# Flamingo-style gated cross-attention with a routed FFN on one core: root iterations on GpSimd, softmax quarters folded into ScalarE, a later fill of the sorted rows, other unit sizes and a new written-out order

## The reference, cut to what matters

```python
x = x + tanh(g_xattn[0]) * xattn(layernorm(x), ctx_768, ...)   # softmax(q k^T / sqrt(16)) v, then wo
x = x + tanh(g_ffn[0]) * ffn(layernorm(x), ...)
# layernorm: (x - mean) / sqrt(var + 1e-5)
# ffn: top1 = argmax of 2 gate scores per token
#   masked[e] = x for tokens of expert e, 0 for the others
#   sum over e of relu(masked[e] @ w1[e] + b1[e]) @ w2[e] + b2[e]     (256 -> 1024 -> 256)
#   + relu(x @ sw1 + sb1) @ sw2 + sb2                                 (shared layers)
```

## Time and profile before

| | us |
|---|---|
| runs before, median (lowest to highest) | 377.28 (376.28 to 381.96), 3 runs |
| the profiled execution: its own time | 374.43 |
| its span in the trace | 372.7 |
| PE busy | 337.0 (90% of the span) |
| DVE, ACT, POOL busy | 246.0, 213.1, 189.9 |

### The profile page before, as it was taken

How to read it: one execution, slowest core, us unless ns; L and a number is a source line. 1 busy time by engine, 2 the same in 40 slices (tenths; PEclk the granted TensorE clock), 3 DMA queues, 4 the chain that set the end, 5 groups by cost and what they waited for, 6 DMA issues and landing times.

```text
span 372.7 us, 7238 instructions
## 1 busy us (share of the span) xinstructions
PE 337.0 (90%) x2337; PEld 304.5 (82%) x2337; DVE 246.0 (66%) x560; ACT 213.1 (57%) x420; POOL 189.9 (51%) x207
## 2 busy tenths in 40 slices
PE   4997189899799999999999798999999999999990
PEld 4665168687698888898889687999999999999980
DVE  5569768888997997977596688632444544445440
ACT  1464488765676764737575375445466554765540
POOL 9194549873526637658252008624454534644342
PEclk9599569999999999999999999999999999999996
DMA  7999375617402242002224011021123112222120
GB/s 191 320 243 335 83 203 150 156 27 198 98 6 82 51 106 75 0 16 99 69 81 146 1 59 57 22 92 37 49 85 84 57 29 73 60 58 66 28 85 28
DMA packets 42935, 34.51 MB, mean 93 GB/s; under 512 B 19370, under 2 KB 40397, under 8 KB 42909
## 3 DMA queue, kind: packets, MB, share of 16 engines
q1 hardware_dynamic: 39210, 26.35, 26.5%
q0 software_dynamic: 2864, 7.17, 6.0%
q10 hardware_dynamic: 835, 0.67, 0.7%
HBM read 22.35 MB, written 12.35 MB: 93 GB/s over the span
## 4 chain that ended last, share of the span: by engine, by line
PE 54%; DVE 14%; SPq 7%; DMA 7%; issue 7%; ACT 4%; POOL 3%; POOLq 2%; DVEq 0%; ACTq 0%
PE y_ps L1360 21%; PE h_ps L1360 13%; PE s_ps L1360 9%; PE bank L1360 6%; DMA stage<-in_L_ffn_w 3%; SPq L522 3%; PE bank L1486 2%; DVE ew_lo L1259 2%; DMA stage<-in_L_ffn_sw 2%; DMA x_all<-in_x 2%; DVE rsum L1150 2%; SPq L447 2%; DVE other_sum L1118 1%; POOLq L659 1%; DVE smax L1132 1%
## 5 line engine op out<-in xcount | busy, mean ns | idle before, releaser
L1326 DVE TENSOR_TENSOR hT_lo<-h,hT_hi 128x256 fp32r<-128x256 f32 x72 | 33.4, 463 | 42.9 <-ACT h L999 42.7
L666 POOL TENSOR_TENSOR probs<-probs,rinv 128x616 f32<-128x616 f32 x32 | 39.2, 1229 | 36.6 <-DVE rinv L1154 35.7
L694 POOL TENSOR_TENSOR hT_lo<-h,hT_hi 128x512 fp32r<-128x512 f32 (+1 forms) x25 | 28.7, 1160 | 25.6 <-ACT h L916 25.5
L1360 PE MATMUL y_ps<-ew_hi,hT_hi 128*128 128x256 f32 x144 | 41.4, 288 | 0.0
L1360 PE MATMUL y_ps<-ew_hi,hT_lo 128*128 128x256 f32 x144 | 40.3, 280 | 0.0
L1360 PE MATMUL y_ps<-ew_lo,hT_hi 128*128 128x256 f32 x144 | 40.3, 280 | 0.0
L1360 PE MATMUL y_ps<-sw_hi,hT_hi 128*128 128x256 f32 x128 | 37.5, 293 | 1.8 <-POOL hT_lo L694 1.8
L996 ACT ACTIVATE hT_hi<-h_ps,vec_cols 128x256 fp32r<-128x256 f32 x36 | 17.1, 476 | 33.8 <-PE h_ps L1360 33.8
L1360 PE MATMUL bank<-pT,v_diag 128*128 128x256 f32 (+1 forms) x160 | 36.3, 381 | 0.0
L1360 PE MATMUL y_ps<-sw_hi,hT_lo 128*128 128x256 f32 x128 | 36.1, 282 | 0.0
L1360 PE MATMUL y_ps<-sw_lo,hT_hi 128*128 128x256 f32 x128 | 36.1, 282 | 0.0
(11 more groups left out here) (186 smaller groups left out, 1086.3 us busy)
## 6 DMA issues: line engine op xcount, KB each, us to landing
v_diag<-v_rows SPq DMA_DIRECT2D x8, 512.0 KB
stage<-in_L_ffn_w SPq DMA_DIRECT2D x4, 1024.0 KB, 6.1
sorted_dram<-empty_rows SPq DMA_DIRECT2D x10, 257.0 KB, 8.5
xs<-sorted_dram SPq DMA_DIRECT2D x10, 257.0 KB, 2.8
stage<-in_L_ffn_sw SPq DMA_DIRECT2D x2, 1024.0 KB, 6.1
x_all<-in_x SPq DMA_DIRECT2D x1, 1536.0 KB, 10.2
part_dram<-x_all SPq DMA_DIRECT2D x3, 512.0 KB, 2.9
k_dram<-probs SPq DMA_DIRECT2D x8, 154.0 KB, 5.5
```

The costliest lines, as they stand in the source:

```text
L666: nc.gpsimd.tensor_tensor(pq, pq, rinv[:, b % 2, k, :].unsqueeze(2).to_broadcast([P, HG, KEYS]), ALU.mult).then_inc(p_ready, 1)
L694: nc.gpsimd.tensor_tensor(hT[1][:, q % HB, 0:width], h32[:, q % 2, 0:width], hT[0][:, q % HB, 0:width], ALU.subtract).then_inc(h_lo_pool, 1)
L1326: nc.vector.tensor_tensor(hT[1][:, c % HB, 0:RTOK], h32[:, c % 2, 0:RTOK], hT[0][:, c % HB, 0:RTOK], ALU.subtract).then_inc(h_lo, 1)
L1360: return nc.tensor.matmul(out_, lhsT, rhs, start=start, stop=stop, **kw)
```

## The change

- The eight batches are grouped for the shared layers as 1, 1, 2, 2, 2 in place of 1, 2, 2, 2, 1.
- The Newton steps and the shift of the second layer norm (all five units) and of the third group of the first (twelve tiles) go from DVE to POOL. DVE keeps the statistics and the three instructions of the first guess. One root is 14 POOL instructions (12 for the steps, 2 for the shift), each waiting for the one before.
- For the 13 quarters in `FOLDED`, DVE does not subtract; it writes the negated maximum, and ACT takes the exponents straight from PSUM, one instruction of 77 columns for each of eight heads, with the maximum as bias. PE then waits for the exponents before it writes these banks again. The scale 1/4 moves into the queries.
- Of each unit's eight low parts two (chunks 1 and 7) are left on POOL in place of five.
- The fill of the sorted rows moves in SP's list from the front to behind `wd.2`; the zeros for the values are two steps with a semaphore each.
- All five lists are written anew; ten warm-up matmuls in place of eight. `wh.0` stands behind `ex.1.1` in ACT's list, where it stood behind `ex.0.1`. The context transposes `yt` stand ahead of the vectors' transpose `vt`.

In the diff, `PE_ORDER` and `ACT_ORDER` are cut to their first lines (and PE's last), and DVE's list is left out.

```diff
+POOL_ROOT = 4 * NEWTON + 2
...
-WARM = 8
-UNITS = [[0], [1, 2], [3, 4], [5, 6], [7]]
+WARM = 10
+UNITS = [[0], [1], [2, 3], [4, 5], [6, 7]]
...
-LO_ON_POOL = (2, 3, 4, 5, 7)
-SORTED_BANK = 1
+LO_ON_POOL = (1, 7)
+FOLDED = {0, 2, 11, 16, 20, 21, 22, 23, 26, 27, 28, 30, 31}
+SORTED_BANK = 0
 PE_ORDER = """
-    warm vt yt.0 yt.1 yt.2 yt.3 kp.0.0 kp.0.1 kp.1.0 in.0.0 kp.1.1 qy.0.1 vp.0 sc.0.0 sc.0.1 vp.1 in.1.0 vp.2
-    vp.3 sc.0.2 qy.1.1 sc.0.3 tn.0.0.0 tn.0.1.1 tn.0.2.0 tn.0.3.1 tn.0.4.0 in.2.1 sc.1.0 sc.1.1 qy.2.0 in.3.1
-    sc.1.2 sc.1.3 va.0.0 qy.3.1 sc.2.0 ou.0.0 in.4.1 sc.2.1 tn.1.0.0 tn.1.1.1 qy.4.0 tn.1.2.1 sc.2.2 tn.1.3.0
-    tn.1.4.1 in.5.0 sc.2.3 va.1.1 tn.2.0.0 sc.3.0 tn.2.1.0 ou.1.1 qy.5.0 sc.3.1 tn.2.2.1 tn.2.3.0 tn.2.4.1
...
+    warm yt.0 yt.1 yt.2 yt.3 vt kp.0.0 in.0.0 kp.0.1 kp.1.0 qy.0.1 kp.1.1 sc.0.0 sc.0.1 vp.0 vp.1 vp.2 vp.3
+    in.1.0 sc.0.2 sc.0.3 tn.0.0.1 qy.1.0 tn.0.1.1 in.2.1 qy.2.0 sc.1.0 sc.1.1 in.3.1 tn.0.2.0 tn.0.3.0 sc.1.2
+    tn.0.4.1 sc.1.3 qy.3.0 in.4.1 qy.4.1 sc.2.0 in.5.0 sc.2.1 va.0.0 tn.1.0.1 sc.2.2 tn.1.1.1 ou.0.0 tn.1.2.1
+    sc.2.3 tn.1.3.1 tn.1.4.0 qy.5.1 sc.3.0 va.1.0 tn.2.0.1 sc.3.1 tn.2.1.1 ou.1.0 tn.2.2.1 sc.3.2 tn.2.3.1
+    tn.2.4.0 n2.0.0.1 va.2.0 h.0.0 tn.3.0.1 sc.3.3 h.0.1 h.0.2 ct.0.0 ou.2.1 h.0.3 y.0.0 h.0.4 y.0.1 h.0.5
...
+    tn.7.1.0 y.2.4 y.2.5 ou.6.0 y.2.6 n2.3.1.1 y.2.7 tn.7.2.0 tn.7.3.1 h.3.0 tn.7.4.0 h.3.1 ct.3.1 va.7.0 h.3.2
+    y.3.0 ou.7.1 h.3.3 h.3.4 y.3.1 y.3.2 h.3.5 h.3.6 y.3.3 h.3.7 y.3.4 y.3.5 y.3.6 n2.4.0.0 n2.4.1.1 y.3.7 oth.0
+    h.4.0 h.4.1 ct.4.1 h.4.2 h.4.3 y.4.0 h.4.4 y.4.1 h.4.5 y.4.2 h.4.6 y.4.3 h.4.7 y.4.4 y.4.5 xst.0 y.4.6 y.4.7
 """
 ACT_ORDER = """
-    vce yte.0 yte.1 wqhi yte.2 nm.0 yte.3 tanh k32.0.0 wohi khi.0.0 ine.0.0 k32.0.1 k32.1.0 khi.0.1 k32.1.1
-    khi.1.0 khi.1.1 q32.0.1 vpe.0 nm.1 vpe.1 ine.1.0 ex.0.0 ex.0.1 q32.1.1 qe.1 wh.0 ex.0.2 te.0.0.0 ex.0.3
-    te.0.1.1 te.0.2.0 te.0.3.1 nm.2 te.0.4.0 nm.3 ine.2.1 vpe.2 nm.4 wh.1 ex.1.0 q32.2.0 nm.5 qe.2 ex.1.1
...
+    yte.0 yte.1 wqhi yte.2 vce nm.0 yte.3 ine.0.0 wohi k32.0.0 khi.0.0 k32.0.1 q32.0.1 khi.0.1 tanh k32.1.0
+    k32.1.1 khi.1.0 nm.1 khi.1.1 ex.0.0 vpe.0 ex.0.1 vpe.1 ine.1.0 te.0.0.1 ex.0.2 te.0.1.1 q32.1.0 ex.0.3 qe.1
+    nm.2 nm.3 ine.2.1 nm.4 q32.2.0 qe.2 ine.3.1 te.0.2.0 nm.5 ex.1.0 te.0.3.0 ex.1.1 te.0.4.1 wh.0 ine.4.1
+    ex.1.2 nm.6 q32.3.0 ex.1.3 qe.3 nm.7 ine.5.0 ex.2.0 vpe.2 q32.4.1 ex.2.1 vae.0.0 te.1.0.1 wh.1 te.1.1.1
...
 POOL_ORDER = """
-    klo.0.0 bi.0 klo.0.1 klo.1.0 klo.1.1 va_.0 bi.1 va_.1 di.0.0 di.0.1 ql.1 di.0.2 di.0.3 bi.2 va_.2 bi.3 bi.4
-    di.1.0 bi.5 ql.2 di.1.1 di.1.2 ql.3 di.1.3 bi.6 di.2.0 di.2.1 ql.4 di.2.2 bi.7 va_.3 di.2.3 di.3.0 di.3.1
-    ql.5 di.3.2 di.3.3 hl.2 hl.3 hl.4 di.4.0 di.4.1 di.4.2 ql.6 hl.5 di.4.3 scat.0 hl.7 di.5.0 di.5.1 ql.7
-    di.5.2 scat.1 hl.10 di.5.3 hl.11 hl.12 di.6.0 hl.13 di.6.1 hl.15 scat.2 di.6.2 di.6.3 hl.18 hl.19 di.7.0
-    di.7.1 di.7.2 hl.20 hl.21 di.7.3 hl.23 scat.3 hl.26 hl.27 hl.28 hl.29 scat.4 hl.31 hl.34 hl.35 hl.36 hl.37
-    hl.39
+    klo.0.0 klo.0.1 bi.0 klo.1.0 bi.1 klo.1.1 va_.0 di.0.0 va_.1 di.0.1 rp.0 rp.1 rp.2 di.0.2 rp.3 ql.1 bi.2
+    di.0.3 bi.3 ql.2 bi.4 di.1.0 bi.5 di.1.1 bi.6 di.1.2 ql.3 va_.2 bi.7 di.1.3 di.2.0 di.2.1 ql.4 di.2.2 ro.0.0
+    ro.0.1 di.2.3 ro.0.2 di.3.0 ro.0.3 va_.3 ro.1.0 di.3.1 ro.1.1 ro.1.2 di.3.2 ro.1.3 ql.5 hl.1 scat.0 di.3.3
+    scat.1 di.4.0 hl.7 di.4.1 di.4.2 ql.6 hl.9 ro.2.0 ro.2.1 di.4.3 ro.2.2 ro.2.3 di.5.0 di.5.1 hl.15 di.5.2
+    ql.7 di.5.3 scat.2 di.6.0 hl.17 di.6.1 di.6.2 di.6.3 di.7.0 ro.3.0 ro.3.1 ro.3.2 ro.3.3 di.7.1 di.7.2 hl.23
+    di.7.3 hl.25 scat.3 ro.4.0 ro.4.1 ro.4.2 ro.4.3 hl.31 hl.33 scat.4 hl.39
 """
 SP_ORDER = """
-    fl vz kw.1 kw.0 wd.0 vw.0 kr.1 wd.1 vw.1 vr.0 kr.2 vw.2 vr.1 wd.2 kr.3 vw.3 vr.2 kr.4 vw.4 vr.3 wd.3 vw.5
-    vr.4 kr.5 vw.6 vr.5 kr.6 vw.7 ps.0 vr.6 kr.7 ps.1 vr.7 wd.4 wd.5 ps.2 xs ps.3 ps.4
+    kw.0 vz.0 vz.1 kw.1 kr.1 vw.0 wd.0 kr.2 vr.0 vw.1 wd.1 kr.3 vr.1 vw.2 wd.2 fl vr.2 vw.3 kr.4 vr.3 vw.4 wd.3
+    kr.5 vr.4 vw.5 vw.6 kr.6 vr.5 ps.0 vw.7 vr.6 kr.7 ps.1 vr.7 wd.5 wd.4 ps.2 ps.3 xs ps.4
 """
 
 
@@ -151,8 +147,9 @@
 LO_POOL = lo_count(CHUNKS_SHARED - 1, True)
 
 
-def unit_of(b):
-    return next(u for u, batches in enumerate(UNITS) if b in batches)
+def folded_count(quarter):
+
+    return sum(n < quarter for n in FOLDED)
 
...
-            def zero_values():
+            def zero_values(n):
 
                 sp.wait_ge(cleared[2], 1)
                 sp.wait_ge(x_in[2], 16)
                 full = CHUNKS - 1
-                for n in range(2):
-                    sp.dma_start(v_dram[n, 0:full * P].rearrange("(c p) g f -> p c (g f)", p=P),
-                                 v_diag[:, 0, 0:full, :, :].rearrange("p c g f -> p c (g f)")).then_inc(v_zeroed, 16)
-                    sp.dma_start(v_dram[n, full * P:GK].rearrange("p g f -> p (g f)"),
-                                 v_diag[0:ROWS[full], 0, full, :, :].rearrange("p g f -> p (g f)")
-                                 ).then_inc(v_zeroed, 16)
+                sp.dma_start(v_dram[n, 0:full * P].rearrange("(c p) g f -> p c (g f)", p=P),
+                             v_diag[:, 0, 0:full, :, :].rearrange("p c g f -> p c (g f)")).then_inc(v_zeroed[n], 16)
+                sp.dma_start(v_dram[n, full * P:GK].rearrange("p g f -> p (g f)"),
+                             v_diag[0:ROWS[full], 0, full, :, :].rearrange("p g f -> p (g f)")).then_inc(v_zeroed[n], 16)
 
             def keys_out(half):
 
...
+            def refine(var_mean, r, n, moved, tiles, done, count, part):
+
+                v, t, r_ = n[:, 0, tiles], n[:, 1, tiles], r[:, tiles]
+                if part < NEWTON:
+                    nc.gpsimd.tensor_tensor(t, v, r_, ALU.mult).then_inc(done, 1)
+                    pool.wait_ge(done, count + 1)
+                    nc.gpsimd.tensor_tensor(t, t, r_, ALU.mult).then_inc(done, 1)
+                    pool.wait_ge(done, count + 2)
+                    nc.gpsimd.tensor_scalar(t, t, -0.5, 1.5, ALU.mult, ALU.add).then_inc(done, 1)
+                    pool.wait_ge(done, count + 3)
+                    nc.gpsimd.tensor_tensor(r_, r_, t, ALU.mult).then_inc(done, 1)
+                    pool.wait_ge(done, count + 4)
+                else:
+                    mean = var_mean[:, tiles, 0:1].rearrange("p t o -> p (t o)")
+                    nc.gpsimd.tensor_tensor(t, mean, r_, ALU.mult).then_inc(done, 1)
+                    pool.wait_ge(done, count + 1)
+                    nc.gpsimd.tensor_scalar(moved[:, tiles], t, -1.0, None, ALU.mult).then_inc(done, 1)
+
+            def refine1(part):
+
+                if part == 0:
+                    pool.wait_ge(seeds1, 3)
+                tiles = slice(TB * LN_GROUPS[2][0], TB * (LN_GROUPS[2][-1] + 1))
+                refine(mv, rstd, nt, shift, tiles, root1[2], 4 * part, part)
+
+            def refine2(u, part):
+
+                if part == 0:
+                    pool.wait_ge(seed2, 3 * (u + 1))
+                tiles = slice(TILE0[u], TILE0[u] + UNIT_TILES[u])
+                refine(mv2, rstd2, nt2, shift2, tiles, root2, POOL_ROOT * u + 4 * part, part)
...
-                act.wait_ge(root1[(0, 1, 2)[min(b, 2)]], ROOT_OPS)
+                act.wait_ge(root1[min(b, 2)], ROOT_OPS if b < 2 else POOL_ROOT)
...
+                                               bias=bq_sb[:, g:g + 1], scale=HEAD_DIM ** -0.5)
...
-                act.wait_ge(s_shifted, 4 * b + k + 1)
-                nc.scalar.activation(probs[:, b % 2, k, :], probs[:, b % 2, k, :], ACT.Exp, scale=HEAD_DIM ** -0.5
-                                     ).then_inc(p_exp, 1)
+                quarter = 4 * b + k
+                to = probs[:, b % 2, k, :]
+                if quarter not in FOLDED:
+                    act.wait_ge(s_shifted, quarter + 1 - folded_count(quarter))
+                    nc.scalar.activation(to, to, ACT.Exp).then_inc(p_exp, 1)
+                    return
+                act.wait_ge(s_max, quarter + 1)
+                if b == 1:
+                    act.wait_ge(k_out[0], 16 * 4)
+                    act.wait_ge(k_out[1], 16 * 4)
+                if b >= 2:
+                    act.wait_ge(pT_ps, TURNS * (b - 1))
+                for h in range(HG):
+                    keys = slice(h % HH * KEYS, (h % HH + 1) * KEYS)
+                    ins = nc.scalar.activation(to[:, h * KEYS:(h + 1) * KEYS], score_banks(quarter)[:, h // HH, keys],
+                                               ACT.Exp, bias=smax[:, b % 2, k, h:h + 1])
+                ins.then_inc(p_exp, 1)
 
...
+            def statistics2(u):
+
+                dve.wait_ge(stats2_rdy, UNITS[u][-1] + 1)
+                tiles = unit_tiles(u)
+                for t in range(tiles.start, tiles.stop):
+                    ins = nc.vector.bn_aggr(mv2[:, t, :], stats2[:, t, :])
+                ins.then_inc(var2_ready, 1)
+
+            def seeds(var, r, n, tiles, done, count):
+
+                v = n[:, 0, tiles]
```

(32 more changed lines are left out.)

112 lines of the change are left out of this document (49 added, 63 removed).

## The result

The changed kernel takes 382.29 us (median of 4 runs, 379.22 to 384.84) beside 378.44 us for the kernel before (4 runs, 376.28 to 381.96). The ratio is 1.0116, with a 95% interval of 1.0059 to 1.0172. So it is a little slower, within the 2% that count as the same; I had forecast 365.3 us and a range that ended at 373. The profiled execution took 382.51 us, its span is 380.7.

What follows compares the result with a forecast made beforehand. PE's own work was taken as the bound, leaving at most 19.6 us idle, the start's idle and the clock's cost to win. Terms -7 + 0.5 - 2 + 0.5 - 2.5 + 0.5 - 1 - 1 = -12.0 took 377.3 to 365.3 us, range 355 to 373.

Steps and rivals of the forecast that it cites:

- The fill and `wh.0`, -7: Front: with the fill off SP's head and `wh.0` later, batch 1's scores start 4 to 13 us earlier; gain 7, range 3 to 10.
- The fill in its new place, +0.5: Ahead of `vr.2` and `kr.4`: the fill's issue and landing are just covered; cost 0.5 us, range 0 to 6.
- rival B: The fill collides: `vr.2`, `kr.4` and later values come late for batches 2 to 4; costs 6 us, 371; chance 0.12.
- The clock, -1: 32 to 60 us: less work runs at the lower clock, granted at 0.76; gain 1 us, range 0 to 3.
- My bound, 3.9 us: 32 to 60 us: the most that 16.4 us of PE work at 0.76 clock can hide.
- 60 to 100, -2: 60 to 100 us: DVE loses net 12 us of work, mostly in 60 to 210; PE idle falls 2 us, range 0 to 3.5.
- the root, +0.5: Root chain on POOL: 5.1 us with the guesses, 2.5 longer, mostly covered by other PE work; cost 0.5 us, up to 5.
- Rival C: Small POOL instructions are dear, 0.95 + 0.07 us each, a chain 14.3 us; about 20 us in all, 385; chance 0.07.
- The start, -1: Start: PE's 3.43 us wait for the vectors shrinks as context transposes go first; gain 1 us, range -0.5 to 4.
- End of the shared layers, -2.5: 210 to 260 us: PE's waits for unit 3's root and a POOL low part shrink; gain 2.5 of 3.7, range 0 to 3.5.
- folding, +0.5: Folded quarters: eight exponents take 2.0 us for 0.72 on ACT, banks held longer; cost 0.5 us, range 0 to 6.
- Rival D: The front gains little: `kr.1` stays at 44 us and `wh.0` blocks ACT as before, only later; 370; chance 0.11.

Runs made afterwards that it cites:

- the three pairs: Kernels with and without folded exponents: changed kernel 1.0116 and 1.0068; fill in front 0.9888 and 0.9950; that with 10 and 17 filler matmuls 0.9778 and 0.9843.
- the dummies: 10 and 17 matmuls with unread results added in PE's two waits: changed kernel with the fill in front 0.9778, with the fill kept 0.9951.
- the three attempts to reorder: Changed kernel, steps moved in POOL's and ACT's lists, fill late: 0.9945; `wl.0` earlier, fill in front: 0.9943; that plus POOL and ACT moves: 0.9969.
- fill_behind_keys4: Changed kernel with the fill moved in SP's list from directly behind `wd.2` to behind the keys of batch 4: 374.01 us, ratio 0.9947.

## Why the prediction was wrong

- **The fill and `wh.0`, -7.** Failed. I credited the fill's leaving. It brought 1.0 us for the first keys in the new order (20.29 to 19.32) and 2.3 in the old (27.05 to 24.74), and no time (0.9947 with the fill late, 0.9888 with it in front). "I put these at 22 to 24 us, between the end of the fills and the 27.05" took SP for the bound; POOL's low parts were. The front did move, by the order: the first scores of batch 1 start at 45.97 us for 50.11, 4.1 us, at the short end of my 4 to 13 (rows below).
- **The fill in its new place, +0.5.** Failed, the largest miss. The term was 8.6 us by the ratios (1.0116 less 0.9888, of 377; 6.4 against the fill late), each give or take 3, for my 0.5 and at or beyond the end of my 0 to 6. The failed step is "the issue at about 71". I had put the fill's 11 us between `wd.2` and `vr.2` and assumed `wd.2` free; it waited 8.2 us for `wl.0`. And I watched `vr.2` and `kr.4`, the loads; the victim was a write, `vw.3`, through an in-order copy that needed its buffer. This is near to rival B, whose condition "if `wd.2` isn't held" I named and did not work out; but no load came late to PE, and B's sign (a wait that ends with `v_diag` or `k_hi` landing) did not show.
- **The clock, -1.** Failed in sign. I took most of the low clock to be in the idle. In the new order two waits stand where one stood, PE works through 20 us of 32 to 60 us, and the granted clock there is 0.57; keeping PE busy in the two waits gains 1.1% with the fill in front, 1.7% with it kept. My bound, 3.9 us, was one for what could be won; I set none for a loss.
- **60 to 100, -2, and the root, +0.5.** The price of a small POOL instruction was near, 0.20 us at 0.28 apart for 0.25 and 0.07, apart from single ones like the 2.12 us below. Rival C is refuted. The worth was too small: taking the roots off DVE is 2.5%, some 9 us, with the fill in front. With the collision it showed as nothing (1.0116 and 1.0113).
- **The start, -1.** Right in kind: the 3.43 us wait for the vectors is gone, two of 1.4 and 1.1 us stand for it. Its worth was not measured alone.
- **End of the shared layers, -2.5; folding, +0.5.** Right: the 3.7 us are gone, and eight exponents took 1.83 us for 2.0, ACT 226.0 us in all for "about 230". Whether the folding costs or gains is not shown: the three pairs differ by 0.5 to 0.7%, not all the same way.
- **The sum.** I had -12 us; the changed kernel's ratio is +4.4. The fill's new place makes some 8 of these 16 us (8.6 for 0.5). The low clock makes some 4 (the gain of the dummies; what it costs the kernel before is open). With both away (0.9778, -8.3 us) about 4 are left that were not taken apart; the front, 4.1 us earlier for 7, lies in them. Rival D has the right size there and the wrong cause: it wanted `kr.1` at 44 us and `wh.0` in ACT's way.

`kr.1` was issued by 37.4 us, and the first scores of batch 1 began only at 45.97. What they stood behind on PE were the transposes and queries of batch 2 (the changed kernel: SP, POOL, ACT, then PE):

```profile
37.01 0.42 SPq L463 DMA_DIRECT2D k_lo<-k_dram  x1
```

```profile
38.51 0.24 POOL L720 TENSOR_SCALAR shift<-nt 128x12 f32<-128x12 f32 x1
```

```profile
39.44 2.08 ACT L860 ACTIVATE xn<-x_all,shift,rstd 128x256 f32<-128x256 f32 x4
```

```profile
40.67 1.09 PE L1497 MATMUL bank<-ident,xn 128*128 128x128 f32 x4 [4.37 <-ACT xn L860]
...
45.97 0.71 PE L1427 MATMUL s_ps<-k_hi,q_stack 128*128 128x308 f32 x2
```

So in this trace the front's bound is the normalising of batch 2, behind the twelve-tile root on POOL and other steps in ACT's list, and then PE's own work at the low clock. The prediction put the keys there.

POOL and DVE got in each other's way at two places (DVE, then POOL, of the changed kernel in order of time):

```profile
68.68 4.57 DVE L1323 TENSOR_TENSOR sw_lo<-stage,sw_hi 128x2048 fp32r<-128x2048 f32 x1
...
84.09 2.29 DVE L1323 TENSOR_TENSOR sw_lo<-stage,sw_hi 128x2048 fp32r<-128x2048 f32 x1
```

```profile
69.89 5.61 POOL L664 TENSOR_TENSOR probs<-probs,rinv 128x616 f32<-128x616 f32 x3
...
84.32 2.12 POOL L708 TENSOR_TENSOR nt<-nt,rstd 128x2 f32<-128x2 f32 x1
```

The small root instruction, 0.20 us elsewhere, began inside DVE's subtraction and ended 0.06 us after it. The Trainium skill, "SBUF — State Buffer", section "Who interferes with whom", says that a VectorE instruction with two inputs in SBUF contends with a GpSimd instruction that reads SBUF. The traces agree: the three divisions beside the first subtraction took 5.61 us where one takes 1.22 elsewhere, and the subtraction 4.57 where it takes 2.29.

## What to carry to other kernels

When a block of transfers is moved in a queue, follow each transfer behind it to every step that waits for it, writes as well as loads, and then to what stands behind that step in its in-order engine; and ask whether the transfer ahead of the block is itself held. Find what makes the first thing behind the block ready before giving the block's length as a gain. And read a matmul engine's busy time with its clock and its count of matmuls beside it: here 20 us of busy time held no more matmuls than 16 did before. 27 matmuls that fill PE's waits gained 1.1 and 1.7%, where they ended as the wait did, and nothing where they ran on; the three attempts to reorder around them gained nothing.

## What was not expected of the hardware

The zero-filling transfers hold up the issues behind them too: two issues of values took 0.82 us alone, 1.56 behind the same loads without a fill (fill_behind_keys4) and 6.13 with it, and their data landed 10.05 us after the second of them began. Two losses need not add: with the fill in its new place the roots' engine made no difference, with the fill in front 2.5%. An experiment that finds nothing while a larger wait stands has shown nothing about the smaller one.
